# Block scales made on ScalarE from the fifth pair on, with the pair behind rounded between the maxima and the reciprocal

## The reference, cut to what matters

```
def fp4_quant_dequant(x):
    xb = x.reshape(shape[:-1] + (shape[-1] // BLOCK, BLOCK))
    scale = jnp.max(jnp.abs(xb), axis=-1, keepdims=True) / 6.0
    scale = jnp.maximum(scale, jnp.float32(1e-12))
    xn = xb / scale
    idx = jnp.searchsorted(_MID, jnp.abs(xn))
    q = _GRID[idx] * jnp.sign(xn) * scale
...
    gate = fp4_linear(x, w_gate)
    y = fp4_linear(x, w_up)
    h = jax.nn.silu(gate) * y
    return fp4_linear(h, w_down)
```

## Time and profile before

| | us |
|---|---|
| median of 3 runs | 146.13 |
| lowest, highest | 145.43, 148.22 |
| the profiled execution, its own time | 145.39 |
| span of the profiled execution, first to last instruction | 143.6 |

### The profile page before, as it was taken

One profiled execution on the slowest core, in us unless ns is written; L12 is line 12 of the kernel. 1 busy time (PEld: TensorE's weight loads), 2 busy tenths in 40 slices (PEclk: granted clock), 3 DMA queues, 4 the chain that ended last, 5 costly groups with the idle time before them and its releaser, 6 DMA issues. The chain is left out here.

```text
span 143.6 us, 2120 instructions
## 1 busy us (share of the span) xinstructions
PE 112.5 (78%) x641; PEld 83.9 (58%) x641; DVE 128.7 (90%) x222; ACT 93.3 (65%) x199; POOL 110.7 (77%) x127
## 2 busy tenths in 40 slices
PE   4505799431966699899989998999899899998783
PEld 4403245211533668586757876785767587787672
DVE  0899999999999995999999999999999999999950
ACT  3979865925786469828984983698377426662632
POOL 3668996982559979997999799889979995838220
PEclk9985699975589999999999999999999999999999
DMA  4970000000000000100010010001000100100102
GB/s 151 310 282 2 0 2 0 2 0 0 2 0 0 5 0 0 73 0 5 22 51 0 0 73 7 2 0 73 0 0 0 73 5 0 73 0 5 73 0 73
DMA packets 2890, 4.90 MB, mean 34 GB/s; under 512 B 448, under 2 KB 832, under 8 KB 2880
## 3 DMA queue, kind: packets, MB, share of 16 engines
q1 hardware_dynamic: 2736, 4.77, 9.3%
q10 hardware_dynamic: 144, 0.00, 0.1%
HBM read 2.67 MB, written 2.10 MB: 33 GB/s over the span
## 5 line engine op out<-in xcount | busy, mean ns | idle before, releaser
L774 PE MATMUL ps_g<-wg_T,xq_T 128*128 128x352 f32 x64 | 27.2, 509 | 9.7 <-ACT silu L624 9.5
L624 ACT ACTIVATE silu<-ps_g 128x352 f32<-128x352 f32 x32 | 14.7, 459 | 17.5 <-PE ps_g L774 17.5
L830 PE MATMUL ps_o<-wd_T,hq_T 128*128 128x128 f32 x174 | 24.2, 275 | 0.0
L449 POOL TENSOR_TENSOR hq<-hn,den 128x704 f32<-128x704 bf16 x15 | 20.8, 1385 | 3.9 <-DVE hn L1016 3.9
L783 PE MATMUL ps_u<-wu_T,xq_T 128*128 128x352 f32 x64 | 23.1, 482 | 0.0
L830 PEld LDWEIGHTS ps_o<-wd_T,hq_T 128*128 128x128 f32 x174 | 22.1, 194 | 0.0
L634 ACT ACTIVATE big<-ps_u 128x704 bf16<-128x704 f32 (+1 forms) x17 | 12.3, 723 | 12.8 <-DVE ps_u L1004 12.7
L774 PEld LDWEIGHTS ps_g<-wg_T,xq_T 128*128 128x128 f32 x64 | 10.2, 198 | 15.2 <-ACT silu L624 13.7
L809 PEld LDWEIGHTS ps_h<-ident,hq 128*128 128x128 f32 x96 | 12.3, 143 | 10.3 <-issue 4.6
L630 ACT COPY hq_T<-ps_h 128x384 f32<-128x384 f32 x32 | 15.1, 473 | 4.4 <-PE ps_h L809 4.4
L809 PE MATMUL ps_h<-ident,hq 128*128 128x128 f32 x96 | 16.1, 278 | 2.3 <-POOL hq L449 1.0
(11 more groups left out here) (157 smaller groups left out, 257.5 us busy)
## 6 DMA issues: line engine op xcount, KB each, us to landing
x_all<-x_in SPq DMA_DIRECT2D x8, 256.0 KB, 6.1
out<-x_all SPq DMA_DIRECT2D x7, 256.0 KB, 2.0
w_raw<-w_in SPq DMA_DIRECT2D x1, 560.0 KB, 5.8
out<-x_all SPq DMA_DIRECT2D x1, 128.0 KB, 1.7
out<-x_all SPq DMA_DIRECT2D x2, 64.0 KB, 1.5
par<-params_in ACTq DMA_DIRECT2D x1, 3.5 KB, 3.0
```

Of the source, the lines that this page charges most:

```text
L449: pool.tensor_tensor(hq_blocks(q), hn_blocks(q), pair_scales(den[q % 4]), ALU.mult).then_inc(s_hq, 1)
L624: act.activation(silu[q % 2][:, j, :], ps_g[:, 0:I], ACT.Silu).then_inc(s_silu, 1)
L774: pe.matmul(ps_g[:, 0:I], x_cols(t), wg_T[:, :], start=True, stop=True).then_inc(s_gate, 1)
L830: m = pe.matmul(o, hq_T[t % 3][:, c * P:(c + 1) * P], wd_T[:, c, :], start=False, stop=(c == NCH - 1))
```

## The change

From q = 4 (the fifth pair, `SETTLED`) to q = 14 the kernel works in another way; the first four pairs and the last are as before. `late(q)` says which.

- `den` is no longer made by VectorE in one operation but by ScalarE in two: `above` = relu(maxima x 1/6 - tiny), then `den` = `above` + tiny (a function `scales` on ScalarE). VectorE only takes the reciprocal (`inverses`), when `s_den` says that `den` is there.
- VectorE's shift and shift back of pair q - 1 move from the head of the iteration q to between the maxima and the reciprocal.
- TensorE's order in the iteration changes: `sum_parts` of tile a moves ahead of `turn_h(b)`, and the up pair moves behind the sums of both tiles.
- ScalarE's `big_x` (odd pairs) moves ahead of the first `copy_hT`.
- GpSimd's `shift_back_x` (odd pairs) moves ahead of `scale_h`. `demodulate_re` moves from the end of an odd iteration to the head of the next, which is the same place in the sequence.

```
+        SETTLED = 4
+        def late(q):
+            return SETTLED <= q < LAST
...
 @@ GpSimd
                         modulate_re(g)
                         if g + 2 < NG:
                             shift_x(g + 2, 1, 0, GT)
+                            if late(q):
+                                shift_back_x(g + 2, 1, 0, GT)
...
                     if g + 2 < NG:
-                        shift_back_x(g + 2, 1, 0, GT)
+                        if not late(q):
+                            shift_back_x(g + 2, 1, 0, GT)
                         scale_x(g + 2, 1, 0, GT)
 @@ ScalarE
+            def scales(q):
+                n = HBP + (XBG if with_x(q) else 0)
+                act.wait_ge(s_ham, q + 1)
+                if with_x(q):
+                    g = q // 2 + 2
+                    act.wait_ge(s_xam, g + 1)
+                    act.wait_ge(s_xq, x_done(g - 2))
+                act.activation(above[:, 0:n], maxima(q)[:, 0:n], ACT.Relu, scale=NUDGE / 6,
+                               bias=neg_tiny_c).then_inc(s_above, 1)
+                act.wait_ge(s_above, n_late(q))
+                act.wait_ge(s_hq, q - 3)
+                act.activation(den[q % 4][:, 0:n], above[:, 0:n], ACT.Identity, bias=tiny_c).then_inc(s_den, 1)
...
                     if g % HALVES:
                         turn_state(g - 1)
+                    if late(q):
+                        scales(q)
                     if g + 1 < NG:
                         copy_xqT(g + 1, 1, 0, GT)
...
                         silu_tile(2 * q + 2)
+                    if late(q) and g + 2 < NG:
+                        big_x(g + 2, 1, 0, GT)
                     if q >= 2:
                         copy_hT(2 * q - 4)
-                    if q > 1 and g + 2 < NG:
+                    if late(q):
+                        scales(q)
+                    elif q > 1 and g + 2 < NG:
                         big_x(g + 2, 1, 0, GT)
 @@ VectorE
+            def inverses(q, x):
+                n = HBP + (XBG if x else 0)
+                dve.wait_ge(s_den, n_late(q))
+                if x:
+                    dve.wait_ge(s_xv, x_done(q // 2 + 1))
+                dve.reciprocal(inv[q % 2][:, 0:n], den[q % 4][:, 0:n]).then_inc(s_rc, 1)
...
-                if q > 0:
+                if q > 0 and not late(q):
                     shift_h(q - 1, 0, 0, PAIR)
                     shift_back_h(q - 1, 0, 0, PAIR)
                 product(q)
...
-                scales(q, with_x(q))
+                if late(q):
+                    shift_h(q - 1, 0, 0, PAIR)
+                    shift_back_h(q - 1, 0, 0, PAIR)
+                    inverses(q, with_x(q))
+                else:
+                    scales(q, with_x(q))
                 divide_h(q)
```

More of the change, by code:

```diff
@@ L77, in build @@
         ident = sb("ident", [P, P])
-        consts = sb("consts", [P, 4])
+        consts = sb("consts", [P, 6])
+        above = sb("above", [P, HBP + XBG])
         steps = sb("steps", [P, GT + 1], I32)
@@ L203, in build @@
         s_ham = sem("h_amax_ready")
+        s_above = sem("h_scales_above_tiny")
+        s_den = sem("h_scales_ready")
         s_rc = sem("h_inverses_ready")
@@ L237, in build @@
         first_re, first_im, neg_turn = col(18), col(19), col(20)
-        base_c, quarter_c, round_c, unround_c = (consts[:, n:n + 1] for n in range(4))
+        base_c, quarter_c, round_c, unround_c, tiny_c, neg_tiny_c = (consts[:, n:n + 1] for n in range(6))
         X_COLS = slice(HBP, HBP + XBG)
@@ L285, in build, with n_late, inverted @@
         LAST = NP - 1
+        SETTLED = 4
+        def late(q):
+            return SETTLED <= q < LAST
+        def n_late(q):
+            return min(max(q + 1 - SETTLED, 0), LAST - SETTLED)
+        def inverted(q):
+            return 2 * (q + 1) - n_late(q)
         def parts(q):
@@ L318, in _ @@
             pool.memset(ident[:, :], 0.0).then_inc(s_idz, 1)
-            for c, value in ((base_c, BASE), (quarter_c, math.pi / 2), (round_c, ROUND), (unround_c, -ROUND)):
+            for c, value in ((base_c, BASE), (quarter_c, math.pi / 2), (round_c, ROUND), (unround_c, -ROUND),
+                             (tiny_c, TINY * NUDGE), (neg_tiny_c, -TINY * NUDGE)):
                 pool.memset(c, value).then_inc(s_const, 1)
@@ L379, in divide_x @@
                 else:
-                    pool.wait_ge(s_rc, 4 * g - 6)
+                    pool.wait_ge(s_rc, inverted(2 * g - 4))
                 if g >= 3:
@@ L477, in _ @@
                     elif g > 0:
+                        if g > 2:
+                            demodulate_re(g)
                         modulate_im(g - 1)
@@ L497, in _ @@
                     if g + 2 < NG:
-                        shift_back_x(g + 2, 1, 0, GT)
+                        if not late(q):
+                            shift_back_x(g + 2, 1, 0, GT)
                         scale_x(g + 2, 1, 0, GT)
-                    if 0 < g < NG - 1:
-                        demodulate_re(g + 1)
+                    if g == 1:
+                        demodulate_re(2)
             pool.wait_ge(s_hn, done(LAST, 0))
@@ L515, in whole_turns @@
             def whole_turns():
-                act.wait_ge(s_const, 4)
+                act.wait_ge(s_const, 6)
                 act.wait_ge(s_turns, 1)
@@ L853, in _ @@
                     gate_tile(2 * q + 3)
+                if late(q):
+                    sum_parts(a, out_cols(a))
                 if q >= 2:
                     turn_h(b)
-                if q >= 4 and q % 2 == 0 and q // 2 + 1 < NG:
+                if late(q) and q % 2 == 0 and q // 2 + 1 < NG:
                     turn_xq(q // 2 + 1, 1, 0, GT)
-                if q < LAST:
+                if q < LAST and not late(q):
                     up_pair(q + 1)
@@ L862, in _ @@
                 if q >= 2:
-                    sum_parts(a, out_cols(a))
+                    if not late(q):
+                        sum_parts(a, out_cols(a))
                     sum_down(a, out_cols(a))
@@ L866, in _ @@
                     sum_down(b, out_cols(b))
+                if late(q):
+                    up_pair(q + 1)
                 if q % 2 == 0 and q // 2 + 1 < NG:
@@ L997, in scales @@
                                   ALU.max).then_inc(s_rc, 1)
-                dve.wait_ge(s_rc, 2 * q + 1)
+                dve.wait_ge(s_rc, inverted(q) - 1)
+                dve.reciprocal(inv[q % 2][:, 0:n], den[q % 4][:, 0:n]).then_inc(s_rc, 1)
[4 more added lines that the diff above has]
+                    dve.wait_ge(s_xv, x_done(q // 2 + 1))
                 dve.reciprocal(inv[q % 2][:, 0:n], den[q % 4][:, 0:n]).then_inc(s_rc, 1)
             def divide_h(q):
-                dve.wait_ge(s_rc, 2 * q + 2)
+                dve.wait_ge(s_rc, inverted(q))
                 for j0, j1 in parts(q):
```

## The result

| | before | after |
|---|---|---|
| median | 147.18 us (4 runs, same chip) | 162.84 us (4 runs) |
| lowest, highest | 145.43, 148.24 | 162.81, 162.97 |
| profiled execution, span | 145.39, 143.6 | 162.97, 161.2 |

The ratio is 1.117 (95% interval 1.1125 to 1.1219): slower by 11.7%. I forecast slower, by 8.5 us on the profiled execution, with a range of 150 to 157. It was 17.6 us, twice that, and all four times lie above the range. Some executions of the kernel before take 147.8 to 149.4 us by themselves and the others 145.2 to 146.5, and the ratios leave out the disturbed ones.

The account below looks back on a forecast made before the run. VectorE (13.42 us per group) and the `y_im` loop (13.30) were taken as near-equal bounds. The loop's 5.4 us, a 2.1 us first delay and changes in the last pairs made 8.5: 145.39 + 8.5 = 153.9 us, range 150 to 157.

Parts of the forecast that it names:

- the chain: Even pairs: `y_im`, TensorE's sum, turn of `hq`, ScalarE's copy, `den`, then VectorE's reciprocal; 2.1 us delay at pair 4.
- the loop: From one group's `y_im` through TensorE, ScalarE and GpSimd to the next; grows from 13.30 to 14.65 us per group.
- at most 0.1 us a group: Most that savings on VectorE can be worth unless the `y_im` loop shrinks too; 13.42 against 13.30 us.
- small activations at 0.33 us: ScalarE's two new operations per late pair, 0.33 us each, 0.66 us from maxima to `den`.
- the sum of the late stage: Adding up delays over the late pairs: reciprocal of pair 14 at 135.35 instead of 126.85, 8.5 us later.
- first wait for `den`: VectorE's reciprocal of pair 4 starts at 63.41 instead of 61.33, a delay of 2.1 us.
- four steps of `y_im`: From `y_im` of group 1 to that of group 5, four times 1.35 us longer, 5.4 us.
- pairs 12 to 14: Stretch between those reciprocals: shorter VectorE pairs, 0.5 us of scan waits and 1.05 us more at pair 14; 0.8 us.
- the term of the three operations: TensorE, even pairs: turn of `hq`, turn of `xq` and up pair queued behind the `y_im` wait, +1.7 us.
- The faster one: Rival: VectorE stays the bound and keeps its 5.9 us saving, giving 139.5 us; chance 0.06.
- The second: Rival: first delay of 2.1 us comes, but groups stay at 13.3 us; 147 to 149 us, chance 0.14.
- The third: Rival: as forecast, plus late ScalarE `scales` in odd pairs, 0.5 to 1 us each; 157 us or more, chance 0.04.

Follow-up runs that it names:

- turn_before_sum: Changed kernel, with the turn of `hq` put ahead of the sum that waits for `y_im` in late pairs; 155.08 us, ratio 1.062.
- tensor_order_alone: Kernel before, with only TensorE's new order in pairs 4 to 14; 165.08 us, ratio 1.122.
- gaps_filled_not_last: Changed kernel, with 16 extra identity transposes in the waits for `y_im` at pair 2 and even late pairs except pair 14; 156.25 us, ratio 1.071.
- filled_waits: Changed kernel, with 16 extra identity transposes in the waits for `y_im` at pair 2 and every even late pair; 156.82 us, ratio 1.077.
- tensor_old_order: Changed kernel, with TensorE's order of before and all other edits kept; 150.65 us, ratio 1.031.
- den_and_shifts: Kernel before, with VectorE's shifts moved and `den` made on ScalarE in pairs 4 to 14; 149.87 us, ratio 1.031.
- none_late: Changed kernel with no late pair, only the small edits left; 145.59 us, ratio 0.999.
- shifts_and_gap_filled: Kernel before, with VectorE's shifts moved, `den` kept there, and 16 identity transposes ahead of pair 2's first sum; 144.6 us, ratio 0.995.
- before_gap_filled: Kernel before, with 16 extra identity transposes ahead of the first sum of pair 2; 146.2 us, ratio 1.007.

## Why the prediction was right, and where it failed

**Right: the direction, the chain and the loop.** TensorE's first sum, put ahead of the turn of `hq` and the up pair, waits for `y_im` and holds up both. `turn_before_sum` takes the chain to `den` away, and with it most of the waits for `den`; `tensor_order_alone` shows that this order makes the loss without any other edit. The periods at full clock are 14.88 us; I had 14.65. That what VectorE saves is worth "at most 0.1 us a group" held: with `den` kept on VectorE and the shifts moved, the step went from 13.42 to 13.31 us and was stopped there by `y_im`.

**Right: small activations at 0.33 us.** They took 0.28 to 0.36. The Trainium skill, "ScalarE: Activation LUTs", section "Rules for kernel authors", would rather have this on VectorE. The runs agree with its sign, though not for the reason of its price: on ScalarE two operations of 0.33 us cost some 4.4 us over the kernel, and 2.5 to 3.5 us came back when they stood elsewhere in the same queue.

**Wrong: the size.** The step that failed is the sum of the late stage: it puts the clock at nothing, for it prices every TensorE instruction with durations of a trace whose clock was 1.00 in this stage, while the same text lets TensorE idle "some 2 to 3 us right after the gate matmul" in every group. I never asked what such a wait does to the granted clock. The reciprocal of pair 14 is 17.5 us late, and it divides so:

| term | forecast | at full clock | in the profile after |
|---|---|---|---|
| first wait for `den` | 2.1 | 2.2 | 2.2 |
| four steps of `y_im` | 5.4 | 6.3 | 9.5 |
| pairs 12 to 14 | 0.8 | 1.3 | 2.7 |
| `y_im` of group 1 | 0 | 0 | 2.7 |
| sum | 8.5 | 10.0 | 17.5 |

(What is left, 0.2, 0.2 and 0.4 us, stands at pair 12: before, its reciprocal started 0.19 us ahead of the end of `y_im`, that of pair 4 0.04 us behind it.) The third column is from `gaps_filled_not_last` and `filled_waits`; the fourth from the rows above: steps 62.72 to 125.44 less 4 x 13.30; reciprocals 129.12 to 144.38, 15.26, less 12.53. About 1.5 us of the error is thus a loop and an end that I sized too small. In the loop it is the term of the three operations, 1.7 us: from the end of `y_im` to the silu it took 5.62 us (63.98 to 69.60) and before 3.66 (61.29 to 64.95), 1.96 more. `big_x` ahead of the copy gave back 0.39, near the 0.36 of the forecast. What made the end 0.5 us longer isn't broken down.

The clock behind the new waits took 4.6 us: 3.2 in two groups and 1.4 in pairs 12 to 14 (granted 0.51 from 128 to 131). `filled_waits` shows it as cause and not only as company: with more instructions and a clock of 1.00 the 3.2 us are gone, and `gaps_filled_not_last` gets back the 1.4 as well.

The last 2.7 us lie before `y_im` of group 1, ahead of the late pairs. Of these, 1.3 stands already at `y_im` of group 0 (47.93 against 46.67), where the clock rose between 42 and 44 us and not between 40 and 42. The other 1.4 follows a gap of TensorE of 2.09 us that ended at 49.31, after which the clock was 0.50 from 50 to 52. The kernel before has the same gap of 2.09 us, ending at 48.04, and its clock stayed at 1.00 there. So this part was in the comparison of two executions, and the forecast had no term for it.

**Wrong without harm here: `den` on ScalarE.** I priced its lateness only on the `y_im` chain. With TensorE's old order it is late as well (`tensor_old_order`, `den_and_shifts`), some 4.5 us that the prediction didn't have anywhere. In the changed kernel only reciprocals of even pairs wait for it, those behind `y_im`, so I don't count it in the miss.

**Rivals.** The faster one needed `y_im` 2.1 us ahead of the reciprocal; it fell with the first wait. The second fell with the periods of 14.87. The third (157 or more, through late `scales` in odd pairs) would have matched the time, but not the mechanism: no reciprocal of an odd pair waits in the changed kernel, and ScalarE waits for the maxima in one odd pair only, pair 13 (0.64 us at 135.42), and in none of the four where the rival needed it.

**Open.** The stage before the late pairs is hardly touched by the change, and `none_late`, which has the same small edits, took the time of before. How late this stage ends differs between profiled executions of kernels with the same order there: `y_im` of group 0 starts at 46.58 in `shifts_and_gap_filled` and at 47.98 in `before_gap_filled`. The four times of the changed kernel, within 0.16 us of each other, suggest that all of them lost the 2.7 us, but only one was profiled, and no run tells why. Nor does any tell why one wait loses the clock and the next doesn't.

## What to carry to other kernels

Before an instruction that waits is moved forward in an in-order queue, list what is now behind it and whose loop that closes; a second loop 1% shorter than the first one decides as much as the first. And wherever a forecast lets TensorE idle for a few microseconds in each round, price the work behind the wait at half the clock too: here that was 4.6 us of the 17.5, a quarter of the loss. Moving two cheap operations to an engine with room is free only where they come before its next long queue, not because its busy share is low.

## What the runs showed of the hardware

- In the late pairs a wait of TensorE of 2.2 to 3.1 us was followed, in some rounds and not in others, by about 3 us at 1.2 GHz, 1.4 to 1.6 us lost each time. The 3.11 us wait that ended at 64.05 wasn't followed by a fall and the 2.19 us one that ended at 78.92 was, so the wait's length alone doesn't decide.
- 16 transposes of the identity put into the waits kept the clock at 1.00 and made a kernel with more instructions 6.0 us faster, some 4.8 us of it behind the first of them. With one such set ahead of the first sum of pair 2, none of 11 executions of two kernels took over 146.8 us (`before_gap_filled`, `shifts_and_gap_filled`); without it, 4 of 10 of the kernel before on that chip took 147.9 or more.
- ScalarE's operations on 128 x 44 and 128 x 76 elements took 0.28 to 0.33 and 0.30 to 0.36 us: the size made about 0.03 us.
